# Scores of two attention heads in 64-row tiles of TensorE, in place of one zero-padded 96-row stack

## The reference

```python
h = layernorm(x) * (1 + scale) + shift            # scale, shift, gate from the condition
q, k, v = heads(h @ Wqkv + b)
a = softmax(q @ k.T * hd ** -0.5)                 # layer 1: causal; layer 2: no scale, / D ** 0.5 after
x = x + gate * ((a @ v) @ Wo + bo)
h2 = layernorm(x) * (1 + scale2) + shift2
x = x + gate2 * (gelu(h2 @ W1 + b1) @ W2 + b2)    # layer 2: x + sln(x)
```

## Time and profile before

| | |
|---|---|
| median of 3 runs | 1216.07 us (1214.62 to 1216.55) |
| the profiled execution | 1208.6 us, its span 1206.8 us |
| mean granted clock of TensorE in it | 0.976 of full speed |
| PE, DVE, ACT, POOL busy | 92%, 68%, 46%, 15% of the span |
| matmuls | 7540, each with its load |

### The profile page before, as it was taken

One profiled execution on the slowest core, in us unless ns is written; L12 is line 12 of the kernel. 1 busy time (PEld: TensorE's weight loads), 2 busy tenths in 40 slices (PEclk: granted clock), 3 DMA queues, 4 the chain that ended last, 5 costly groups with the idle time before them and its releaser, 6 DMA issues.

```text
span 1206.8 us, 22214 instructions
## 1 busy us (share of the span) xinstructions
PE 1107.2 (92%) x7540; PEld 843.7 (70%) x7540; DVE 814.8 (68%) x2245; ACT 554.2 (46%) x1120; POOL 180.1 (15%) x290
## 2 busy tenths in 40 slices
PE   6799999999999999999999888888888999999996
PEld 4567777777777777777777665555555777777765
DVE  5566677666677667766667677777778656776642
ACT  1235655555543455444455334444444446555451
POOL 5011111101102211011111001111114101011010
PEclk9679999999999999999999999999999999999998
DMA  7713332123343333312333413333343233322300
GB/s 264 212 48 106 107 106 75 62 76 105 107 150 131 93 107 106 94 58 66 103 107 116 130 57 113 113 110 113 106 154 119 64 99 116 116 72 67 92 25 18
DMA packets 102714, 123.18 MB, mean 102 GB/s; under 512 B 8992, under 2 KB 96032, under 8 KB 101600
## 3 DMA queue, kind: packets, MB, share of 16 engines
q1 hardware_dynamic: 102048, 121.73, 32.5%
q10 hardware_dynamic: 576, 0.30, 0.1%
HBM read 85.16 MB, written 35.78 MB: 100 GB/s over the span
## 4 chain that ended last, share of the span: by engine, by line
PE 70%; DVE 14%; issue 5%; DMA 5%; ACT 4%; ACTq 1%; SPq 0%; POOL 0%; DVEq 0%; POOLq 0%
PE dense L1162 12%; PE dense L1148 10%; PE dense L1093 9%; PE s_bank L1186 9%; PE o_bank L1241 8%; PE st_bank L1223 7%; DMA q_stack<-max_t 5%; DVE neg_max L793 4%; PE o_bank L1122 3%; PE o_bank L1108 2%; PE o_bank L1072 2%; PE s_bank L1196 2%; PE o_bank L1248 2%; ACT xn L553 2%; DVE s_bank L788 1%
## 5 line engine op out<-in xcount | busy, mean ns | idle before, releaser
L605 ACT ACTIVATE probs<-st_bank 128x512 f32<-128x512 f32 (+1 forms) x512 | 263.9, 568 | 263.3 <-PE st_bank L1223 202.7
L793 DVE TENSOR_REDUCE neg_max<-s_bank 128x2 f32<-128x512 f32 x384 | 256.3, 684 | 65.8 <-PE s_bank L1186 61.7
L1186 PE MATMUL s_bank<-k_stack,q_stack 96*128 96x256 f32 (+1 forms) x1024 | 231.7, 317 | 9.4 <-DVE neg_max L793 1.7
L1186 PEld LDWEIGHTS s_bank<-k_stack,q_stack 96*128 96x128 f32 x1024 | 165.3, 193 | 60.8 <-issue 24.1
L1162 PE MATMUL dense<-w_sb,hid 128*128 128x256 f32 x768 | 201.0, 380 | 0.0
L1223 PE MATMUL st_bank<-q_stack,k_stack 98*128 98x512 f32 x384 | 153.3, 471 | 13.2 <-DMA q_stack<-max_t 12.3
L443 POOL TENSOR_TENSOR veps<-mv,eps_c 128x2 f32<-128x2 f32 x65 | 12.7, 196 | 990.2 <-DVE mv L759 976.0
L1241 PE MATMUL o_bank<-probs,v_aug 128*32 128x256 f32 (+1 forms) x2048 | 133.4, 379 | 22.2 <-ACT v_aug L545 18.2
L1162 PEld LDWEIGHTS dense<-w_sb,hid 128*128 128x128 f32 x768 | 130.5, 189 | 10.7 <-issue 0.4
L1093 PE MATMUL dense<-ht,w_sb 128*128 128x256 f32 x512 | 128.3, 391 | 4.3 <-DVE row_out L745 3.2
L593 ACT ACTIVATE hid<-dense,vec 128x256 f32<-128x256 f32 x192 | 80.6, 471 | 100.9 <-PE dense L1148 100.8
(11 more groups left out here) (120 smaller groups left out, 1502.7 us busy)
## 6 DMA issues: line engine op xcount, KB each, us to landing
q_stack<-qk_dram SPq DMA_DIRECT2D x192, 128.0 KB, 2.9
k_stack<-qk_dram SPq DMA_DIRECT2D x96, 256.0 KB, 4.0
par_sb<-par_dram SPq DMA_DIRECT2D x32, 512.0 KB, 5.6
qk_dram<-q_hi SPq DMA_DIRECT2D x32, 256.0 KB, 2.1
qk_dram<-q_lo SPq DMA_DIRECT2D x32, 256.0 KB, 2.2
qk_dram<-k_hi SPq DMA_DIRECT2D x32, 256.0 KB, 2.2
qk_dram<-k_lo SPq DMA_DIRECT2D x32, 256.0 KB, 2.1
w_sb<-w SPq DMA_DIRECT2D x3, 1280.0 KB, 9.5
```

The costliest lines, as they stand in the source:

```text
L605: nc.scalar.activation(probs[p % 4][:, kt, :, q0:N], src, ACT.Exp, scale=SCORE_SCALE[l]).then_inc(p_sb, 1)
L793: nc.vector.tensor_reduce(neg_max[:, qt, 2 * p:2 * p + 2], split3(bank[:]), AX.X, ALU.max, negate=True).then_inc(s_max, 1)
L1186: ins = mm(bank[:, e * N:e * N + k1], q_stack[g.par][0:KB, 2 * p + e, qt * P:(qt + 1) * P].bitcast(F32R), k_stack[g.par][0:KB, p, 0:k1].bi ...
```

## The change

Each head of a pair has a row tile of TensorE of its own: head e stands in rows 64 e to 64 e + 49 of both stacks, 48 rows of parts and the two rows of the maximum. There are no zeros; `q_stack` has a slot for a pair, not for a head. Its matmuls are built with a tile of 64x128 at rows 0 and 64, where before all of them had 128x128 (and `values` 128x32, as it still has).

Scores come in 8 quads i: two pairs, one query half, four matmuls; head 0 of both pairs in `s_bank[0]`, head 1 in `s_bank[1]`. A quad may start when all maxima of the quads before are done. Tile j of `score_max` is now one bank of a quad. `score_t` of a pair is four matmuls of 256 columns, one bank for each head. In layer 1 the mask comes first, in a full tile, then six matmuls of 128 columns in row tiles. `exps` takes one head at a time (all its keys) instead of one half of the keys. `probs` is laid out for that.

q_hi and k_hi are spilled twice (6 stores of 256 KB instead of 4), in an order that lets `stack` load 48 rows with one DMA: 4 loads instead of 9. `max_rows` has four DMAs of 4 KB instead of two of 8 KB; in steps without an MLP half of them are issued by SP and half by ACT. The first half's `max_turn` writes into `st_bank`. The order on PE and DVE is new. The core of the diff:

```diff
-KB = 3 * 2 * HD
+KB = 3 * HD
 KM = KB + 2
+P2 = P // 2
...
-        q_stack = [sb(f"q_stack{i}", [P, H, N]) for i in range(2)]
+        q_stack = [sb(f"q_stack{i}", [P, PAIRS, N]) for i in range(2)]
...
-        def max_rows(eng, g, half):
+        def max_rows(eng, g, half, members=(0, 1)):
...
-            h0 = half * H // 2
-            for part in range(2):
-                dst = q_stack[g.par][KB + part:KB + part + 1, h0:h0 + H // 2, :]
-                src = max_t[half][part * H // 2:(part + 1) * H // 2, :]
-                eng.dma_start(dst, src).then_inc(max_ld, 16)
+            p0, n = half * PAIRS // 2, PAIRS // 2
+            for e in members:
+                for part in range(2):
+                    r0, row = (2 * part + e) * n, e * P2 + KB + part
+                    eng.dma_start(q_stack[g.par][row:row + 1, p0:p0 + n, :], max_t[half][r0:r0 + n, :]).then_inc(max_ld, 16)
...
             def stack(a):
...
+                for which, stacks, spilled in ((0, q_stack, q_spill), (1, k_stack, k_spill)):
+                    wait(sp, spilled, a.count(48, 48))
+
+                    src = qk_dram[a.par, which].rearrange("t (j r) part n -> (r part) (t j) n", j=4)
                     for e in range(2):
...
+                        dst = stacks[a.par][e * P2:e * P2 + KB]
+                        sp.dma_start(dst, src[e * KB:(e + 1) * KB]).then_inc(stack_ld, 16)
...
-            def fill_stack(i):
-                nc.gpsimd.memset(q_stack[i][:], 0.0).then_inc(q_filled, 1)
...
-                        wait(pe, s_max, g.count(16, j - 1))
...
+            def score(g, *quads):
+
+                for i in quads:
+                    p0, qt = i // 2 * 2, i % 2
+                    wait(pe, s_max, g.count(16, 4 * i // 2))
...
+                    for p in (p0, p0 + 1):
+                        for e in range(2):
+                            rows = slice(e * P2, e * P2 + KB)
+                            c0 = (p - p0) * N
+                            ins = mm(s_bank[e][:, c0:c0 + k1],
+                                     q_stack[g.par][rows, p, qt * P:(qt + 1) * P].bitcast(F32R),
+                                     k_stack[g.par][rows, p, 0:k1].bitcast(F32R), start=True, stop=True)
...
             def score_t(g, *pairs):
...
+                    for e in range(2):
+                        wait(pe, p_sb, g.count(16, 2 * p - 1 + e))
+                        if CAUSAL[g.layer]:
+
+                            mm(split3(st_bank[e][:])[:, :, 0:P], ident_b[:], mask_k[:], start=True, stop=False)
+                        else:
+                            mm(st_bank[e][:, 0:N], *stacks(g, p, e, 0, 0, N), start=True, stop=True)
                     if CAUSAL[g.layer]:
...
+                        for e in range(2):
+                            mm(st_bank[e][:, 0:P], *stacks(g, p, e, 0, 0, P), start=False, stop=False)
+                        for e in range(2):
+                            mm(st_bank[e][:, N:N + P], *stacks(g, p, e, 1, P, N), start=False, stop=True)
+                        for e in range(2):
+                            mm(st_bank[e][:, P:N], *stacks(g, p, e, 0, P, N), start=True, stop=True).then_inc(st_ps, 1)
                         continue
...
+                    for e in range(2):
+                        mm(st_bank[e][:, N:2 * N], *stacks(g, p, e, 1, 0, N), start=True, stop=True).then_inc(st_ps, 1)
```

More of the change, by code:

```diff
@@ L154, in cond_seq_blocks @@
         max_t = [sb(f"max_t{i}", [H, N]) for i in range(2)]
-        probs = [sb(f"probs{i}", [P, T, 2, N]) for i in range(4)]
+        probs = [sb(f"probs{i}", [P, 2, T, N]) for i in range(4)]
         o_sb = [sb(f"o_sb{i}", [P, N]) for i in range(2)]
@@ L353, in step @@
                 mlp = c.exists and HAS_MLP[c.layer]
+                if not mlp and g.off > 0:
+                    max_rows(sp, g, 0, (1,))
                 if inputs_of(a):
@@ L356, in step @@
                     stack(a)
+                if not mlp and g.off > 0:
+                    max_rows(sp, g, 1, (1,))
                 if g.reg is None:
@@ L1262, in step @@
                     score_t(g, 0)
+                    score(g, 5)
                     if inputs:
@@ L1373, in step @@
                     values(g, 3)
-                    score(a, 6)
+                    max_turn(a, 0)
                     out_turn(g, 3)
-                    score(a, 7)
-                    ao_turn(g)
                     if n.exists:
                         ht1_t(n)
-                    max_turn(a, 0)
+                    ao_turn(g)
                     if modulated:
@@ L1401, in _ @@
             products(Step(1))
-            score(first, *range(8))
+            score(first, 0, 1, 2, 3)
             max_turn(first, 0)
```

224 lines of the change are left out of this document (88 added, 136 removed).

## The result

The changed kernel takes **1363.02 us** (median of 4 runs, 1360.95 to 1368.24) where the kernel before takes 1215.34 (4 runs beside it): a ratio of 1.122, 95% interval 1.1185 to 1.1256. It is slower, as forecast, but by 148 us and not by 65; the time lies outside the range.

A forecast was written before the change was run, and what follows sets the result against it. TensorE (PE) was taken as the bound, its order being the path at MLP steps. 15 x 2.0 + 8 x 3.0 + 8 x 1.5 - 1 = +65 us on the 1216.07 median gave 1281, stated as 1280; range 1180 to 1320.

The forecast's parts named there:

- the term for the steps without an MLP: Eight steps without an MLP: shorter start -1.0, later rows of maxima +2.5, so +1.5 each (0 to 3), 12 us.
- What a change of tile shape costs: TensorE switching between row, column and full tiles: 0.1 us gap plus 0.1 exposed weight load, 0.20 us per change.
- The rival without gaps: Changes of tile shape on TensorE cost nothing, only the waits remain: +25 us, 1240; chance 0.15.
- Two row tiles at once: TensorE's scores and transposed scores: two row-tile matmuls share one 0.12 us slot; a quad 0.24, a pair's transposed scores 0.24.
- The rival of serial loads: Row tiles load weights one after the other, slots take 0.24 us, not 0.12: +75 on the forecast, 1355; chance 0.08.
- PE's own sum: TensorE in a non-causal MLP step: 3.7 us saved by row tiles, 3.2 added by 16 changes of shape, net -0.5.
- The wait at quad 7: First half of a non-causal MLP step: TensorE waits 1.3 us for VectorE's maximum 13; `values(1)` ends 1.9 later.
- +2.0 for the step: Whole non-causal MLP step: first half +1.9 us, second half +0.1, together +2.0 (0.5 to 3).
- the sign that I had named for being wrong: In MLP steps: the forecast is wrong if the steps shrink, that is, if quad 7 finds maximum 13 done.
- t4: Transposed scores of pair 4, second half of an MLP step: wait 1.0 us for rows of maxima, four DMA issues.
- The causal term: Eight causal MLP steps: masks add changes of shape, less wait at quad 7 is new; +3.0 us each (1.5 to 5).
- Start: Kernel start and step 0: dropped `q_stack` memsets -4.4 us, quads in series 3 x 0.6, more DMA issues 1.3: -1.

The follow-up runs named there:

- e9: Changed kernel with its own six spills and DRAM layout, but twelve stack loads of 16 rows three apart instead of four of 48 adjacent rows: 1296.9 us.
- e5: Changed kernel with the stack DMAs of the kernel before: four spills for six, twelve loads of 16 rows for four of 48: 1288.08 us.
- e12: Kernel before, with extra 256-column matmuls on 64 rows (64x128 tiles) inserted between full matmuls of `mlp_down`: 1248.24 us.
- e15: e5 plus 16, 8 and 8 unused extra matmuls ahead of the next sequence's first three quads in steps without an MLP: 1259.43 us.
- e13: e7 with maxima over half the keys in the layer without an MLP (outputs differ from the reference's): 1251.76 us.
- e7: e6 plus 16, 8 and 8 unused extra matmuls ahead of the next sequence's first three quads in steps without an MLP: 1263.55 us.
- e3: Changed kernel plus 20, 10 and 10 unused extra matmuls ahead of the next sequence's first three quads in steps without an MLP: 1337.86 us.
- e6: e5 with second-half maxima turned earlier in steps without an MLP, and all four DMAs of their rows issued by ScalarE: 1303.9 us.
- e8: Kernel before, with GpSimd's two memsets of `q_stack` moved behind `xn` of sequences 0 and 1: 1211.91 us.

## Why the prediction was wrong

**The step that failed** is the sentence "Everything new that I costed at nothing (two more spills, fewer and longer stack loads, the new layouts of `probs` and `max_parts`) lies on queues that wait, or keeps its size." I counted bytes and issues, and not where the rows of a load lie in SBUF and how many it has. The loads put back give 66 us (e9), loads and spills together 75 (e5), more than my whole forecast. The sum had no term for it. A second step failed with it: the term for the steps without an MLP, 12 us, had neither TensorE's low clock nor quads that wait for each other's maxima in it, and measured 87.

**What a change of tile shape costs:** right. 0.20 for an entry in the chain (0.43 against 0.23), a gap of 0.1 in both directions (e12 on the way in, the row at 307.40 on the way out). With e12's 0.15 for a change the 16 changes would cost 2.4 us and not 3.2. The rival without gaps fell. (Its sum was also added up wrongly: 15 x 0.5 + 8 x 1.5 + 8 x 1.5 - 1 is +30, so 1246 and not 1240; and the bounds of the terms reach 1324, not 1320. Neither changes the verdict.)

**Two row tiles at once:** right; quad 0.23, pair 0.24 without its entry. The rival of serial loads gave 1355, near the result, for a reason that the chain refutes: a time that fits shows no mechanism.

**PE's own sum, -0.5 per MLP step:** not contradicted, and not measured alone. Its pieces came as priced, and in e5 a step takes 36.6 us before and after, so gain, entries and waits together cancel, where I had +2.0 with the waits.

**The wait at quad 7, 1.3 us, and +2.0 for the step:** wrong in mechanism. In the timeline of VectorE behind the earlier trace rows:

```profile
287.35 0.68 DVE L791 TENSOR_REDUCE neg_max<-s_bank 128x2 f32<-128x512 f32 x1
287.95 1.16 DVE L761 TENSOR_SCALAR xn<-xg,mv,rstd 128x256 f32<-128x256 f32 x2
```

Maximum 11 was to put 0.68 us on this queue. But `xn` now takes 1.16 and not 1.75. Before, all of GpSimd's `addend` ran beside it; now `addend` starts beside maximum 11, which keeps its 0.68. That this overlap sets the length of `xn` is read from the two traces and was not tested (GpSimd's timeline, before and after):

```profile
274.05 1.29 POOL L454 TENSOR_TENSOR xg<-xg,par_sb 128x512 f32<-128x512 f32 x1
```

```profile
287.36 1.28 POOL L453 TENSOR_TENSOR xg<-xg,par_sb 128x512 f32<-128x512 f32 x1
```

Maximum 13 is done at 291.4, one microsecond earlier than I added up (279.2 there lies 9.5 behind the projection's end, here it would be 292.4), and TensorE waits 0.16 us. That is all but the sign that I had named for being wrong, "quad 7 finds maximum 13 done"; yet the steps did not shrink, for another reason. Rows of maxima landed in 3.1 to 4.1 us and not in 1.9, behind the slow loads. In steps 2 to 7 TensorE waited 7.1 us for them and 2.1 in e5, and at `score` 2.0 us for `k_stack` and 1.3 with no releaser named, both nothing in e5: together 1.4 of the 2.0 us a step. The rest is not assigned. The wait for the rows (the window holds seven steps):

```profile
PE st_bank L1211 <- DMA q_stack<-max_t: 7.1, 6, 1.4
```

I forecast 1.0 for t4 and met it by luck: I had it from four issues and not from the queue, and with the old loads, where the issues are the same four, it is 0.35 a step. The causal term, 3.0, is 1.1 in e5 (9.1 in eight steps), and the rest of its 26.1 us is the loads again.

**Steps without an MLP, +1.5:** measured +10.9. It splits in the order in which it was undone: the loads and spills 2.6 a step (e5), the low clock 3.4 (e15), the maxima between quads 1.5 to 1.8 (e13 against e7), and 2.8 of e13's 32.8 us are not accounted for (up to 1 of it may be that its profiled execution was a long one). The order matters: on the changed kernel itself filling was worth 25 us in all (e3), on e5 29 (e15), on e6 40 (e7). I priced one wait, t4's, from a trace in which the granted clock of these steps was 0.99; none of my terms had a clock. I had priced quads in series for the start alone, "3 x 0.6", and left them out in the very steps where no MLP matmuls lie between two quads.

**Start, -1:** measured +4.5. The memset part was right (`xn` back to 2.08 us, `k_lo` earlier), and the first quad of sequence 0 came at 36.97 instead of 41.13. Four quads with their maxima in between, at the low clock, 2.2 us each, ate it (chain of waits; the landing of `k_stack` ahead of them took 9.1 us):

```profile
27.84 9.09 DMA k_stack<-qk_dram
...
36.97 0.57 PE s_bank L1176 x4
37.54 1.29 DVE neg_max L791 x2
...
38.87 0.84 PE s_bank L1176 x4
```

Where the first rows of maxima have landed the two kernels are level (51.41 us, and 51.59 before). The other 4.7 us are lost behind that, in step 0, whose score tiles and maxima also stand in series; no run separates them.

**Still open:** why 48 adjacent rows are slower than 16 rows three apart, what is left of the loss in steps without an MLP, why e6 is slower than e5, and the start, which stays 6.6 us longer in e5 too.

## What to carry to other kernels

When a change keeps a transfer's bytes, look at which partitions it reaches, and how many rows each load has, before pricing it at nothing; and price late landings also for the small transfers that are issued behind the large ones. When a wait is added, ask what TensorE's clock does behind it: here cheap matmuls in such waits gave back 3 to 5 us a step (e3, e15, e7). A step's total that comes out as forecast proves no term of it; undo one part and see whether the total moves as that term says.

## What the runs showed of the hardware

Two DMAs with the same packets and bytes differ in landing by the place of their rows in SBUF: 128 KB to 16 rows three apart 3.4 to 3.6 us, to 16 adjacent rows 4.9 to 7.9. Small DMAs issued behind slow ones land late too: the rows of the maxima took 3.1 to 4.1 us behind loads of 48 adjacent rows, and 1.7 to 2.0 behind loads of 16 rows three apart (steps 2 to 7). Matmuls of 64x128 tiles in one pair of row tiles start together and share a slot of 0.12 us, weight loads included. A matmul of 64 rows between full ones costs 0.27 us more than a full one by the medians, 0.30 by the starts in the trace. And 76 matmuls that compute nothing, with the two memsets moved, made the kernel before 0.8% faster; the memsets alone (e8) can't be told from no change.
